# Expert layer one of a gated cross-attention and MoE block: weight block stationary, 128 moving columns, hidden rows left untransposed

## The chip, the cores and the metric

The kernel runs on one core of one Trainium2 chip. The metric is the device time of one execution in microseconds, lower is better. Three runs of the kernel before took 444.24, 444.64 and 444.83 us (median 444.64).

## What is computed

The input is 32 sequences of 128 tokens with 128 features. A cross-attention stage and a layer norm come first. What the change touches is the mixture of experts after it:

```
probs = softmax(xf @ router_w.T)
topv, topi = top_k(probs, 2); topv = topv / (topv.sum() + 1e-09)
h = gelu(einsum('td,edh->teh', xf, w1))
y = einsum('teh,ehd->ted', h, w2)
out = einsum('te,ted->td', cw, y)
x = x + tanh(g_ffn[0]) * out
```

There are 8 experts, `w1` is 128x512 and `w2` 512x128 for each, and each of the 4096 tokens goes to two of them, so there are 8192 picks. Everything is float32.

## The kernel before, in words

**Attention stage** (`each_step`, the first 55% of the time): per group of four sequences projections, scores, softmax, the product with the values, the router, and GpSimd scatters of normalised token rows into `rows`, sorted by expert. The change leaves it alone.

**Plan**: VectorE works out on the chip how many blocks of 128 rows ("slots") each expert has; `slot_row` and `slot_exp` hold the start row and the expert of each of the 71 slots (64 full ones and 7 spare). Meanwhile ScalarE rounds the first-layer weights to fp32r (`w1h`, L675) and VectorE computes the remainder `w1l = w1 - w1h` (L1013).

**Expert stage** (`each_slot`, `work` on every engine): a software pipeline over the slots. Step `8q + r` handles slot `j` in its first part and earlier slots in the others, by constants called lags. Eight steps are written out, then a rolled loop holds eight per pass, then the rest is written out. Each engine takes its work in the order of the code:

- SyncE loads 128 rows of `rows` into `xg[:, r]`, a ring of eight (L473, L479).
- TensorE, step j: transposes `xg` of slot j into `ps_x` (L1210); runs layer one of slot j-2 (L1220), three matmuls of 512 moving columns, `xh*w1h + xl*w1h + xh*w1l`, with the activations stationary and the weights moving; transposes the four 128-column blocks of `hid` of slot j-3 (L1230); runs layer two of slot j-4 (L1240), four float32 matmuls, each two weight loads and two matmul records in the profile.
- ScalarE rounds the transposed rows into `xh` (L684) and takes the gelu of `ps_score` into `hid` (L691).
- VectorE computes `xl` (L1021), copies `hidT` out of `ps_pT` (L1029, named probT in the profile since it shares that buffer), and scales the result into `yo` (L1035).
- GpSimd runs a one-element add on `pscratch` (L560) and an indirect DMA that scatters `yo` to `picked` (L569).

At `r == 0` TensorE reads the experts of the coming slots into registers (L1186), because its operands are addressed by them. `wait(pe, f_xl, j - 1)` and its like guard the buffers, of which most are double.

**Tail**: the results in `picked` are loaded back, added to `xs` by VectorE (L1043, L1045) and written out.

Of the kernel before, what the change touches and what calls it, by code (L numbers as in the profile page):

```python
# [9 lines left out]
F32R = mybir.dt.float32r  # L10
# [6 lines left out]
D = 128  # L17
# [6 lines left out]
EXPERTS = 8  # L24
HID = 512
HCH = HID // 128
# [26 lines left out]
LAG_UP = 2  # L53
LAG_HT = 3
LAG_DOWN = 4
# [74 lines left out]
def gated_cross_attention_moe(nc, x, ctxT, mask, weights, vectors, w1, w2, ident_c, tables_c,  # L130
                              integers_c, rows, picked, out):
    with ExitStack() as stack:
# [119 lines left out]

        w1h = sb("w1h", [128, EXPERTS, HID], F32R)
        w1l = sb("w1l", [128, EXPERTS, HID], F32R)
        xg = sb("xg", [128, RING, ROW])
# [26 lines left out]
        s_w1 = sem("s_w1")  # L282
        s_ffnw = sem("s_ffnw")
# [60 lines left out]
        s_w1h = sem("s_w1h")  # L344
        s_w1l = sem("s_w1l")
# [3 lines left out]
        f_xl = sem("f_xl")  # L349
        f_up = sem("f_up")  # L350
        f_gelu = sem("f_gelu")
        f_hT = sem("f_hT")
        f_hTs = sem("f_hTs")
# [31 lines left out]
        def seqs(ap):  # L385
            return ap.rearrange("p (b s) -> p b s", b=GROUP)

# [196 lines left out]
        def _(act):  # L584
# [91 lines left out]

            nc.scalar.activation(ascratch[:, :], tgates[:, :], ACT.Gelu)

            def work(q, r):
# [22 lines left out]
        def _(dve):  # L702
# [345 lines left out]
        def _(pe):  # L1048
# [130 lines left out]
            pe.wait_ge(s_w1l, EXPERTS)  # L1179
            pe.wait_ge(s_plan, PLAN)  # L1180

            def experts_of(first, count):

                at = (slot_exp[0:1, first:first + count] if isinstance(first, int)
                      else slot_exp[0:1, bass.ds(first, count)])
                _, values = nc.values_load_multi_w_load_instructions(  # L1186
                    at, engines=[mybir.EngineType.PE], min_val=0, max_val=EXPERTS - 1,
                    skip_runtime_bounds_check_because="the plan takes the minimum with the last expert")
                return [bass.ds(v, 1) for v in values]
# [3 lines left out]
            def work(q, r):  # L1193
                if r == 0:
# [5 lines left out]
                    turn["experts"] = experts_of(first, count)  # L1200
# [11 lines left out]
                if j is not None:  # L1212
# [3 lines left out]
                    e = expert(LAG_UP)  # L1216
                    pe.wait_ge(f_xl, j + 1)
                    wait(pe, f_gelu, j - 1)
                    for a, w, first in ((xh, w1h, True), (xl, w1h, False), (xh, w1l, False)):
                        last = nc.tensor.matmul(ps_score[i][:, :], a[:, (r - LAG_UP) % XRING, :],  # L1220
                                                w[:, e, :].rearrange("p o h -> p (o h)"),
                                                start=first, stop=(w is w1l))
                    last.then_inc(f_up, 1)
                j = slot_of(q, r, LAG_HT)
                if j is not None:
                    i = (r - LAG_HT) % 2
                    pe.wait_ge(f_gelu, j + 1)
                    wait(pe, f_hTs, j - 1)
                    for c in range(HCH):
# [63 lines left out]
```

## Time and profile before

| | value |
|---|---|
| runs, median (lowest to highest) | 444.64 us (444.24 to 444.83) |
| the profiled execution, first to last instruction | 452.3 us |
| PE busy | 358.2 us, 79% |
| DVE busy | 314.0 us, 69% |
| POOL busy | 244.6 us, 54% |
| ACT busy | 206.1 us, 46% |
| TensorE clock granted, mean | 0.927 |

The profile is of one execution. Its own time is known only as its span, 452.3 us, which is 7.7 us above the median of the runs without a profile; a change in time worked out in the span is carried over to the median unchanged. Busy times of different engines overlap; what bounds a stretch is read from who waits for whom in it.

### The profile page before, as it was taken

To read this page: it belongs to the slowest core of one execution; us is meant where nothing else is said; L and a number is where in the kernel's file an instruction comes from. 1 tells how busy PE (TensorE), PEld (TensorE's weight loads), DVE (VectorE), ACT (ScalarE), POOL (GpSimd) and SP (SyncE) were. 2 spreads that over 40 slices of the span, in tenths; PEclk is the share of its full clock that TensorE was granted. 3 is DMA by queue.
4 is the path that set the end of the run, shared out by engine and by line. 5 is a ranking of instruction groups with operands and counts; after the bars stand their busy time and mean duration, and the time that the engine had idled before them with its cause. 6 is when DMAs were issued, how large, how long until landed. Compare 5 with 4: busy or idle time off the path is not lost.

```text
span 452.3 us, 10441 instructions
## 1 busy us (share of the span) xinstructions
PE 358.2 (79%) x2747; PEld 287.1 (63%) x2748; DVE 314.0 (69%) x1059; ACT 206.1 (46%) x506; POOL 244.6 (54%) x302
## 2 busy tenths in 40 slices
PE   2799999989878898887553029999999999999800
PEld 2566767766565675664442018989889889898700
DVE  3778789999797997878655645655656656565545
ACT  2176667575655657556413404434333334343200
POOL 3755454528758587585467633555555555555600
PEclk9999999999999999999965559999999999999955
DMA  7224412011121011004511221212212222222079
GB/s 213 72 65 137 143 49 72 27 53 54 50 70 47 31 40 47 21 25 133 143 43 41 78 78 29 67 53 58 58 56 54 62 64 58 54 58 61 22 242 315
DMA packets 41472, 34.42 MB, mean 76 GB/s; under 512 B 5205, under 2 KB 37335, under 8 KB 41441
## 3 DMA queue, kind: packets, MB, share of 16 engines
q1 hardware_dynamic: 32898, 23.49, 18.1%
q0 software_dynamic: 4320, 8.47, 5.6%
q10 hardware_dynamic: 4224, 2.10, 1.6%
q8 instruction: 14, 0.23, 0.2%
q14 instruction: 16, 0.13, 0.1%
HBM read 22.35 MB, written 12.01 MB: 76 GB/s over the span
## 4 chain that ended last, share of the span: by engine, by line
PE 54%; DVE 16%; issue 11%; POOL 7%; DMA 6%; SPq 3%; ACT 2%; DVEq 1%; another core or an unknown queue 0%; POOLq 0%; ACTq 0%
PE ps_score L1220 9%; PE ps_score L1072 8%; PE ps_proj L1240 6%; PE ps_pT L1230 5%; PE ps_o L1240 5%; PE ps_pT L1095 4%; POOL rows L537 3%; PE ps_o L1150 3%; DMA maskbc<-picked 2%; POOL picked L569 2%; DVE rowmax L920 2%; PE ps_proj L1106 2%; PE ps_proj L1110 2%; PE ps_tail L1128 1%; DVE prob L949 1%
## 5 line engine op out<-in xcount | busy, mean ns | idle before, releaser
L523 POOL TENSOR_TENSOR kblk<-kT,tables 128x1024 f32<-128x1024 f32 x32 | 60.6, 1895 | 53.4 <-ACT kT L618 52.9
L569 POOL DMA_INDIRECT picked<-yo,xg x71 | 70.6, 994 | 11.9 <-POOL pscratch L560 11.6
L1029 DVE COPY probT<-ps_pT 128x512 f32<-128x512 f32 x71 | 49.1, 691 | 39.2 <-PE ps_pT L1230 21.9
L537 POOL DMA_INDIRECT rows<-xr,posi x64 | 64.2, 1004 | 16.1 <-issue 15.5
L1072 PE MATMUL ps_score<-kblk,qT 128*128 128x512 f32 x128 | 63.0, 605 | 9.8 <-ACT prob L634 8.4
L560 POOL TENSOR_TENSOR pscratch<-minus_half 1x1 f32<-1x1 f32 x95 | 17.6, 186 | 77.2 <-DVE yo L1035 69.5
L691 ACT ACTIVATE probT<-ps_score 128x512 f32<-128x512 f32 x71 | 42.4, 597 | 33.6 <-PE ps_score L1220 25.9
L607 ACT ACTIVATE probT<-ps_pT 128x512 f32<-128x512 f32 x64 | 35.4, 595 | 40.0 <-PE ps_pT L1095 31.3
L920 DVE TENSOR_REDUCE rowmax<-ps_score 128x4 f32<-128x512 f32 x64 | 41.8, 683 | 8.1 <-PE ps_score L1072 3.8
L1230 PE MATMUL ps_pT<-ident,probT 128*128 128x128 f32 x284 | 42.9, 274 | 0.0
L1230 PEld LDWEIGHTS ps_pT<-ident,probT 128*128 128x128 f32 x284 | 35.7, 141 | 9.8 <-issue 0.2
L1072 PEld LDWEIGHTS ps_score<-kblk,qT 128*128 128x128 f32 x128 | 22.5, 200 | 29.3 <-ACT prob L634 14.8
L638 ACT ACTIVATE prob<-prob 128x512 f32<-128x512 f32 x56 | 33.8, 630 | 9.7 <-DVE prob L949 9.4
L1240 PE MATMUL ps_proj<-w2s,probT 128*128 x288 | 38.1, 275 | 0.0
L1240 PE MATMUL ps_o<-w2s,probT 128*128 x280 | 37.0, 275 | 0.0
L949 DVE TENSOR_TENSOR prob<-ps_score,rowmax 128x512 f32<-128x512 f32 x56 | 36.1, 680 | 0.0
L1240 PEld LDWEIGHTS ps_proj<-w2s,probT 128*128 128x128 f32 x288 | 35.0, 192 | 0.1
L1220 PE MATMUL ps_score<-w1h,xh 128*128 x71 | 34.9, 491 | 0.0
L966 DVE SCALAR_TENSOR_TENSOR qT<-ps_proj,wts,maskbc 64x128 f32<-64x128 f32 x64 | 22.3, 348 | 17.7 <-ACT vals L621 11.2
L1240 PEld LDWEIGHTS ps_o<-w2s,probT 128*128 128x128 f32 x280 | 34.0, 192 | 0.0
L1095 PE MATMUL ps_pT<-ident,prob 128*128 128x128 f32 x256 | 33.2, 273 | 0.0
L684 ACT ACTIVATE xh<-ps_xT 128x128 fp32r<-128x128 f32 x36 | 10.0, 278 | 46.7 <-PE ps_xT L1210 46.7
(142 smaller groups left out, 741.5 us busy)
## 6 DMA issues: line engine op xcount, KB each, us to landing
xg<-rows SPq DMA_DIRECT2D x71, 65.0 KB, 1.8
ctxs<-ctxT SPq DMA_DIRECT2D x32, 128.0 KB, 2.1
xs<-x SPq DMA_DIRECT2D x8, 256.0 KB, 2.9
w1s<-w SPq DMA_DIRECT2D x4, 512.0 KB, 3.4
w2s<-w SPq DMA_DIRECT2D x8, 256.0 KB
w1s<-picked SPq DMA_DIRECT2D x4, 512.0 KB, 5.8
maskbc<-picked SPq DMA_DIRECT2D x4, 512.0 KB, 10.0
out<-xs ACTq DMA_DIRECT2D x8, 256.0 KB, 6.5
```

What stands on the lines that cost most here:

```text
L523: nc.gpsimd.tensor_tensor(kblk[:, r, :, :], kT[:, r, :].unsqueeze(1).broadcast_to([128, HEADS, T]), headmask.unsqueeze(2).broadcast_to([12 ...
L537: nc.gpsimd.indirect_dma_start(out=rows, out_offset=bass.IndirectOffsetOnAxis(ap=posi[:, i, pick, b:b + 1], axis=0), in_=xr[:, i, pick, b, ...
L569: nc.gpsimd.indirect_dma_start(out=picked, out_offset=bass.IndirectOffsetOnAxis(ap=xg[:, r, D + 1:D + 2].bitcast(I32), axis=0), in_=yo[:, ...
L691: nc.scalar.activation(hid[:, i, :, :], heads(ps_score[i][:, :]), ACT.Gelu).then_inc(f_gelu, 1)
L920: nc.vector.tensor_reduce(rowmax[:, r, HALF * h:HALF * (h + 1)], heads(ps_score[h][:, :]), AX.X, ALU.max).then_inc(s_max, 1)
L949: nc.vector.tensor_tensor(prob[:, r, HALF * h:HALF * (h + 1), :], heads(ps_score[h][:, :]), rowmax[:, r, HALF * h:HALF * (h + 1)].unsqueeze(2)
L1029: nc.vector.tensor_copy(hidT[:, i, :, :], heads(ps_pT[i][:, :])).then_inc(f_hTs, 1)
L1072: nc.tensor.matmul(ps_score[h][:, :], qT[:, r, h, :], flat(kblk[:, r, HALF * h:HALF * (h + 1), :]), start=True, stop=True).then_inc(s_sc, 1)
L1095: last = nc.tensor.transpose(ps_pT[h][:, j * T:(j + 1) * T], prob[:, r, HALF * h + j, :], ident[:, :])
L1220: last = nc.tensor.matmul(ps_score[i][:, :], a[:, (r - LAG_UP) % XRING, :], w[:, e, :].rearrange("p o h -> p (o h)"), start=first, stop=(w ...
L1230: last = nc.tensor.transpose(ps_pT[i][:, c * 128:(c + 1) * 128], hid[:, i, c, :], ident[:, :])
L1240: last = nc.tensor.matmul(ps_y[i][:, 0:D], hidT[:, i, c, :], w2s[:, e, c, :].rearrange("p o d -> p (o d)"), start=(c == 0), stop=(c == HCH ...
```

## The change

Layer one is turned around. A block of 128 columns of the weights is the stationary operand, and `xh` or `xl` moves with 128 columns, so that `ps_score` holds the hidden units on the partitions and the tokens along the columns. That is the layout that layer two wants as its stationary operand: the transposes of `hid`, `ps_pT` and the copy to `hidT` are gone. The three terms over four blocks are twelve matmuls. Before each, VectorE copies the expert's `w1h` and `w1l` into a small double buffer `w1c`; for that VectorE now reads `slot_exp` into its own registers at `r == 0`, and its wait for `s_w1l` stands in its own program and no longer in TensorE's. The pipeline is two steps deep and no longer four.

```diff
-LAG_UP = 2
-LAG_HT = 3
-LAG_DOWN = 4
+LAG_UP = 1
+LAG_DOWN = 2
...
+        w1c = sb("w1c", [128, 2, 2, HID], F32R)
...
         hid = probT[:, :, 0:HCH, :]
-        hidT = probT[:, :, HCH:2 * HCH, :]
...
                     act.wait_ge(f_up, j + 1)
-                    wait(act, f_hT, j - 1)
+                    wait(act, f_down, j - 1)
...
+            dve.wait_ge(s_w1l, EXPERTS)
+            turn = {}
 
             def work(q, r):
                 j = slot_of(q, r, 0)
+                if r == 0 and j is not None:
+                    first = RING * q
+                    count = min(RING, SLOTS - first) if isinstance(q, int) else RING
+                    turn["experts"] = experts_of(mybir.EngineType.DVE, first, count)
                 if j is not None:
+                    wait(dve, f_up, j - 1)
+                    for t, w in enumerate((w1h, w1l)):
+                        nc.vector.tensor_copy(
+                            w1c[:, r % 2, t, :],
+                            w[:, turn["experts"][r], :].rearrange("p o h -> p (o h)")).then_inc(f_w1, 1)
                     dve.wait_ge(f_xh, j + 1)
...
-                j = slot_of(q, r, LAG_HT)
-                if j is not None:
-                    i = (r - LAG_HT) % 2
-                    dve.wait_ge(f_hT, j + 1)
-                    wait(dve, f_down, j - 1)
-                    nc.vector.tensor_copy(hidT[:, i, :, :], heads(ps_pT[i][:, :])).then_inc(f_hTs, 1)
...
-            pe.wait_ge(s_w1l, EXPERTS)
...
                     pe.wait_ge(f_xl, j + 1)
+                    pe.wait_ge(f_w1, 2 * j + 2)
                     wait(pe, f_gelu, j - 1)
-                    for a, w, first in ((xh, w1h, True), (xl, w1h, False), (xh, w1l, False)):
-                        last = nc.tensor.matmul(ps_score[i][:, :], a[:, (r - LAG_UP) % XRING, :],
-                                                w[:, e, :].rearrange("p o h -> p (o h)"),
-                                                start=first, stop=(w is w1l))
+                    for c in range(HCH):
+                        for t, a, first in ((0, xh, True), (0, xl, False), (1, xh, False)):
+                            last = nc.tensor.matmul(
+                                ps_score[i][:, c * 128:(c + 1) * 128],
+                                w1c[:, i, t, c * 128:(c + 1) * 128],
+                                a[:, (r - LAG_UP) % XRING, :], start=first, stop=(t == 1))
                     last.then_inc(f_up, 1)
-                j = slot_of(q, r, LAG_HT)
-                if j is not None:
-                    i = (r - LAG_HT) % 2
-                    pe.wait_ge(f_gelu, j + 1)
-                    wait(pe, f_hTs, j - 1)
-                    for c in range(HCH):
-                        last = nc.tensor.transpose(ps_pT[i][:, c * 128:(c + 1) * 128], hid[:, i, c, :],
-                                                   ident[:, :])
-                    last.then_inc(f_hT, 1)
...
-                    pe.wait_ge(f_hTs, j + 1)
+                    pe.wait_ge(f_gelu, j + 1)
                     wait(pe, f_y, j - 1)
                     for c in range(HCH):
-                        last = nc.tensor.matmul(ps_y[i][:, 0:D], hidT[:, i, c, :],
+                        last = nc.tensor.matmul(ps_y[i][:, 0:D], hid[:, i, c, :],
```

How it stands in TensorE's program, one step of the rolled loop of the expert stage. Before (operands are printed as output, moving, stationary; ISA and REGISTER_ALU are register work for addresses and waits):

```order
L1210 MATMUL ps_tail<-ident,xg 128x128
L1220 ISA
L1220 MATMUL ps_score<-w1h,xh 128x512
L1220 MATMUL ps_score<-w1h,xl 128x512
L1220 REGISTER_ALU
L1220 MATMUL ps_score<-w1l,xh 128x512
L1230 MATMUL ps_pT<-ident,probT 128x128 x4
L1240 ISA
L1240 MATMUL ps_o<-w2s,probT 128x128
```

The changed program at the same place (the line numbers are those of the changed file):

```order
L1211 MATMUL ps_tail<-ident,xg 128x128
L1217 REGISTER_ALU
L1218 REGISTER_ALU
L1222 MATMUL ps_score<-xh,w1c 128x128
L1222 MATMUL ps_score<-xl,w1c 128x128
L1222 MATMUL ps_score<-xh,w1c 128x128 x2
L1222 MATMUL ps_score<-xl,w1c 128x128
L1222 MATMUL ps_score<-xh,w1c 128x128 x2
L1222 MATMUL ps_score<-xl,w1c 128x128
L1222 MATMUL ps_score<-xh,w1c 128x128 x2
L1222 MATMUL ps_score<-xl,w1c 128x128
L1222 MATMUL ps_score<-xh,w1c 128x128
```

Three matmuls of 512 columns and four transposes have become twelve matmuls of 128; the transposes that stood between layer one and layer two are gone, and layer two follows at once.

VectorE's program in the rolled loop before, two steps:

```order
L1021 TENSOR_TENSOR xl<-ps_tail,xh 128x128
L1029 COPY probT<-ps_pT 128x512
L1035 TENSOR_SCALAR yo<-ps_o,xg 128x128
L1019 REGISTER_ALU
L1021 TENSOR_TENSOR xl<-ps_xT,xh 128x128
L1029 COPY probT<-ps_pT 128x512
```

And now, at the head of the loop, with the register load of the experts and one step behind it:

```order
L390 TENSOR_LOAD slot_exp
L126 REGISTER_ALU
L1033 ISA
L1033 COPY w1c<-w1h 128x512
L1033 REGISTER_ALU
L1033 COPY w1c<-w1l 128x512
L1036 REGISTER_ALU
L126 REGISTER_ALU
L1038 TENSOR_TENSOR xl<-ps_xT,xh 128x128
L126 ISA
L1046 TENSOR_SCALAR yo<-ps_proj,xg 128x128
```

The copy out of PSUM between `xl` and `yo` is gone, and two copies from SBUF to SBUF stand ahead of `xl`, right behind `yo` of the step before.

## Rows read from the trace of the kernel before

**Rows 1.** The page: span, and the span in 40 slices for TensorE, VectorE and the clock.

```profile
span 452.3 us, 10441 instructions
...
PE   2799999989878898887553029999999999999800
...
DVE  3778789999797997878655645655656656565545
...
PEclk9999999999999999999965559999999999999955
```

**Rows 2.** Busy time by stretch: PE, PEld, DVE, ACT, POOL, then clock, DMA share, GB/s.

```profile
268.30:275.70 7.40, 7.04 (x31) 5.51 (x32) 2.74 (x7) 3.07 (x8) 0.00 (x0) 0.64 0.25 60
299.80:317.40 17.60, 17.56 (x128) 15.79 (x128) 10.52 (x24) 7.00 (x16) 9.41 (x16) 1.00 0.21 59
```

**Rows 3.** The chain of waits in one steady step of the expert stage: start us, us, what.

```profile
302.38 0.11 PE ps_tail L1210
302.49 0.70 PE ps_score L1220 x3
303.19 0.44 PE ps_pT L1230 x4
303.63 0.89 PE ps_o L1240 x8
304.52 0.11 PE ps_xT L1210
```

**Rows 4.** Timeline of weight loads around a step that began after a pause: start us, us.

```profile
282.12 0.14 PEld L1210 LDWEIGHTS ps_xT<-ident,xg 128*128 128x128 f32 x1
282.34 0.19 PEld L1220 LDWEIGHTS ps_score<-w1h,xh 128*128 128x128 f32 x1
282.45 0.19 PEld L1220 LDWEIGHTS ps_score<-w1h,xl 128*128 128x128 f32 x1
282.68 0.19 PEld L1220 LDWEIGHTS ps_score<-w1l,xh 128*128 128x128 f32 x1
```

**Rows 5.** Groups by line, 239 to 430 us: busy us, mean ns, idle before and releaser.

```profile
L1029 DVE COPY probT<-ps_pT 128x512 f32<-128x512 f32 x71 | 49.1, 691 | 39.2 <-PE ps_pT L1230 21.9 <-issue 17.2
L1240 PEld LDWEIGHTS ps_proj<-w2s,probT 128*128 128x128 f32 x288 | 35.0, 192 | 0.1
L560 POOL TENSOR_TENSOR pscratch<-minus_half 1x1 f32<-1x1 f32 x77 | 14.3, 186 | 72.2 <-DVE yo L1035 69.5 <-DVE posi L868 2.6
L1035 DVE TENSOR_SCALAR yo<-ps_proj,xg 128x128 f32<-128x128 f32 x36 | 12.6, 351 | 8.6 <-PE ps_proj L1240 8.6
L1021 DVE TENSOR_TENSOR xl<-ps_xT,xh 128x128 fp32r<-128x128 f32 x36 | 10.5, 291 | 10.2 <-ACT xh L684 8.0 <-issue 0.6
L1013 DVE TENSOR_TENSOR w1l<-w1s,w1h 128x512 fp32r<-128x512 f32 x8 | 4.9, 683 | 0.0
L569 POOL DMA_INDIRECT picked<-yo,xg x71 | 70.6, 994 | 11.9 <-POOL pscratch L560 11.6 <-issue 0.3
```

**Rows 6.** The register load of the experts on TensorE's queue: ns min/median/max.

```profile
L1186 PEldq TENSOR_LOAD <-slot_exp x10: 786/1083/1206, 264.9 to 421.8; - x10
```

**Rows 7.** VectorE groups, 0 to 240 us: SBUF to SBUF with one input.

```profile
L745 DVE TENSOR_SCALAR maskrow<-maskrow 1x4096 f32<-1x4096 f32 x1 | 2.3, 2280 | 1.4 <-DMA maskrow<-mask 1.4
L730 DVE TENSOR_SCALAR wout_g<-wts,tgates 128x256 f32<-128x256 f32 x1 | 0.4, 352 | 2.5 <-ACT tgates L586 2.5
```

**Rows 8.** Timeline, before and in the fill of the expert stage: start us, us.

```profile
259.86 4.90 DVE L1013 TENSOR_TENSOR w1l<-w1s,w1h 128x512 fp32r<-128x512 f32 x8
...
268.36 0.48 PE L1210 MATMUL ps_xT<-ident,xg 128*128 128x128 f32 x1 [15.01 <-DMA xg<-rows]
...
269.18 0.29 DVE L1021 TENSOR_TENSOR xl<-ps_xT,xh 128x128 fp32r<-128x128 f32 x1 [4.42 <-ACT xh L684]
...
271.19 0.41 PE L1210 MATMUL ps_tail<-ident,xg 128*128 128x128 f32 x1
...
272.68 1.03 PE L1230 MATMUL ps_pT<-ident,probT 128*128 128x128 f32 x4
273.53 0.29 PE L1210 MATMUL ps_xT<-ident,xg 128*128 128x128 f32 x1
```

**Rows 9.** Timeline, last input transpose and last layer-two group.

```profile
419.11 0.27 PE L1210 MATMUL ps_xT<-ident,xg 128*128 128x128 f32 x1
...
426.78 1.13 PE L1240 MATMUL ps_proj<-w2s,probT 128*128 x8
```

**Rows 10.** Timeline: VectorE SBUF ops beside a GpSimd multiply, then beside its indirect DMA.

```profile
87.71 1.90 POOL L523 TENSOR_TENSOR kblk<-kT,tables 128x1024 f32<-128x1024 f32 x1 [0.97 <-ACT kT L618]
87.80 1.83 DVE L946 TENSOR_SCALAR nmax<-rowmax 128x4 f32<-128x4 f32 x1
...
209.31 1.15 DVE L984 TENSOR_SCALAR x2n<-xs,nm,rs 128x128 f32<-128x128 f32 x4
...
209.70 1.01 POOL L537 DMA_INDIRECT rows<-xr,posi  x1 [0.16 <-issue]
```

More of the change, by code:

```diff
@@ L251, in gated_cross_attention_moe @@
         pad_row = sb("pad_row", [128, EXPERTS], I32)
+        xg = sb("xg", [128, RING, ROW])
         w1h = sb("w1h", [128, EXPERTS, HID], F32R)
         w1l = sb("w1l", [128, EXPERTS, HID], F32R)
-        xg = sb("xg", [128, RING, ROW])
         xh = sb("xh", [128, XRING, 128], F32R)
         xl = sb("xl", [128, XRING, 128], F32R)
+        w1c = sb("w1c", [128, 2, 2, HID], F32R)
         yo = sb("yo", [128, RING, D])
         hid = probT[:, :, 0:HCH, :]
-        hidT = probT[:, :, HCH:2 * HCH, :]
         yb = [half.rearrange("p (g b k d) -> p g b k d", b=GROUP, k=2, d=D)[:, g]
@@ L282, in gated_cross_attention_moe @@
         s_w1 = sem("s_w1")
+        s_w1h = sem("s_w1h")
+        s_w1l = sem("s_w1l")
         s_ffnw = sem("s_ffnw")
@@ L343, in gated_cross_attention_moe @@
         s_plan = sem("s_plan")
-        s_w1h = sem("s_w1h")
-        s_w1l = sem("s_w1l")
         f_load = [sem(f"f_load{i}") for i in range(RING)]
@@ L349, in gated_cross_attention_moe @@
         f_xl = sem("f_xl")
+        f_w1 = sem("f_w1")
         f_up = sem("f_up")
         f_gelu = sem("f_gelu")
-        f_hT = sem("f_hT")
-        f_hTs = sem("f_hTs")
         f_down = sem("f_down")
@@ L386, in seqs, with experts_of @@
             return ap.rearrange("p (b s) -> p b s", b=GROUP)
+        def experts_of(engine, first, count):
+            at = (slot_exp[0:1, first:first + count] if isinstance(first, int)
+                  else slot_exp[0:1, bass.ds(first, count)])
+            _, values = nc.values_load_multi_w_load_instructions(
+                at, engines=[engine], min_val=0, max_val=EXPERTS - 1,
+                skip_runtime_bounds_check_because="the plan takes the minimum with the last expert")
+            return [bass.ds(v, 1) for v in values]
         block = stack.enter_context(nc.Block())
@@ L1178, in _ @@
             pe.wait_ge(s_ffnw, 16 * EXPERTS)
-            pe.wait_ge(s_w1l, EXPERTS)
             pe.wait_ge(s_plan, PLAN)
[L1182 to L1189, printed above, removed]
             turn = {}
@@ L1199, in work @@
                         count = min(RING * q + RING - LAG_UP, SLOTS) - first
-                    turn["experts"] = experts_of(first, count)
+                    turn["experts"] = experts_of(mybir.EngineType.PE, first, count)
                     turn["first"] = 0 if isinstance(q, int) and q == 0 else -LAG_DOWN
@@ L1215, in work @@
                     i = (r - LAG_UP) % 2
-                    e = expert(LAG_UP)
                     pe.wait_ge(f_xl, j + 1)
+                    pe.wait_ge(f_w1, 2 * j + 2)
                     wait(pe, f_gelu, j - 1)
-                    for a, w, first in ((xh, w1h, True), (xl, w1h, False), (xh, w1l, False)):
-                        last = nc.tensor.matmul(ps_score[i][:, :], a[:, (r - LAG_UP) % XRING, :],
-                                                w[:, e, :].rearrange("p o h -> p (o h)"),
-                                                start=first, stop=(w is w1l))
-                    last.then_inc(f_up, 1)
-                j = slot_of(q, r, LAG_HT)
-                if j is not None:
-                    i = (r - LAG_HT) % 2
-                    pe.wait_ge(f_gelu, j + 1)
-                    wait(pe, f_hTs, j - 1)
-                    for c in range(HCH):
-                        last = nc.tensor.transpose(ps_pT[i][:, c * 128:(c + 1) * 128], hid[:, i, c, :],
-                                                   ident[:, :])
-                    last.then_inc(f_hT, 1)
+                    for c in range(HCH):
[4 more added lines that the diff above has]
+                                a[:, (r - LAG_UP) % XRING, :], start=first, stop=(t == 1))
+                    last.then_inc(f_up, 1)
                 j = slot_of(q, r, LAG_DOWN)
```

## The prediction

> **What bounds the kernel now.** I read the page first: span and slices. TensorE is above 90% busy in every slice of the expert stage, VectorE at five to six tenths, and the clock is full there except in the first steps [rows 1]. Then busy time by stretch: in 17.6 us, eight steps, TensorE is busy for 17.56 us, VectorE for 10.52, GpSimd for 9.41, ScalarE for 7.00 [rows 2]. Then the chain of waits: a steady step is a closed run of TensorE work, 0.11 for the input transpose, 0.70 for layer one, 0.44 for the four transposes of `hid`, 0.89 for layer two, 2.14 us in all [rows 3]. So TensorE's own work bounds the stage, and what counts is what a step costs there; the others have about 0.8 us to spare in each. The attention stage and the tail are untouched.
>
> What bounds TensorE inside a step differs by matmul. Three matmuls of 512 columns in 0.70 us are 0.233 each, 0.020 over 512 columns at 2.4 GHz (0.213): their moving side bounds. The records of 128 columns in layer two come every 0.112 (0.89 / 8) [rows 3]. The decisive row is a weight load with nothing before it to hide it. In a step that began after a pause, the load for `xl*w1h` starts 0.11 us behind the load for `xh*w1h`, and the third only 0.23 later, when the second matmul starts [rows 4]. So a load of 128 fp32r columns takes about 0.11 us at full clock, twice what 128 moving columns need (0.053). The loads of layer two look the same (192 ns against 0.19) and their records come at the same pace [rows 4, 5]. With 512 columns the load is hidden; with 128 it is the longer half.
>
> **The change, term by term.**
>
> TensorE, a steady step. Gone: 3 x 0.233 = 0.70 and four transposes, 0.44; together 1.14. Added: twelve pairs of load and matmul. Their spacing is not in the trace. From below it is bounded by the moving side, 0.233 - 384 / 2400 MHz = 0.073; from above by the float32 price of the same shape, two records, 0.223. I take 0.112, the pace of layer two, because its weight loads have the same form and length and are as long as its moving side: 12 x 0.112 = 1.34. The step becomes 0.11 + 1.34 + 0.89 = 2.34, **0.20 more than now**. The moving columns are as many as before in layer one, 3 x 512; it is the twelve exposed loads that cost more than the transposes saved.
>
> The number of steps. Between the fourth and the last input transpose (slots 3 and 70) lie 67 full steps: 67 x 0.20 = **+13.4 us**. The register load at the head of each pass (about 1.08 us [rows 6], of which 17.6 - 8 x 2.14 = 0.5 shows) stays as it is.
>
> Filling. The first transpose starts at 268.36, when its DMA lands, and the first `xl` is done at 269.5. Layer one of slot 0 can then start. The clock is at 1.2 GHz until about 273.5, where four transposes take 0.85 instead of 0.44 [rows 8]; so twelve pairs take 2.6, to 272.1; transpose 2 takes 0.2; half of layer one of slot 1 takes 1.3 at the low clock and half 0.7 at the full one, to 274.3; layer two of slot 0 ends at 275.1. There transpose 3 starts, which now starts at 271.19: **+3.9**. This is because two lags instead of four put the first layer two ahead of it.
>
> Draining. From the last input transpose to the end of layer two now 419.11 to 427.9, 8.8 us [rows 9]. Then: a step of 2.34, layer one of slot 70 and two layers two, 1.34 + 2 x 0.89, a register load that shows 0.5, and 0.2 for the last matmul to leave: 6.2. **-2.6**.
>
> VectorE. Gone is a copy from PSUM (0.69 [rows 5]). Added are two copies SBUF to SBUF, 128x512. One-input operations there take 352 ns for 256 columns and 2280 for 4096, 0.50 ns a column: 128x512 would be about 0.48 [rows 7]; the upper bound is `w1l`'s 0.68, which come 0.61 apart [rows 5, 8]. A step has 2 x 0.48 + 0.29 + 0.35 = 1.6, at most 2.0, under 2.34: hidden. Behind the copies on its queue stand `xl` and then `yo`; for `xl` of slot j TensorE waits a step later. VectorE's new register load, if like TensorE's 1.08, comes once in eight steps: from the end of a step 0.55 to the end of `yo`, 1.1, two copies 1.0 to 1.2 and `xl` 0.3 are 3.0 to 3.2, against 2.34 + 0.5 + 0.11 = 2.95 at which layer one needs it. Part of the load runs while `yo` does, so I count nothing, and at most 0.3 x 8 = 2 us for the range. If that cover fails, `xl` is late and layer one waits.
>
> GpSimd has 0.18 + 0.16 + 0.99 = 1.33 of 2.34 [rows 5]. ScalarE is unchanged; the gelu of slot j-1 follows layer one and is needed a step later. On SyncE's queue the loads wait for the scatter of eight slots before, which now comes two steps after its transpose and not four: more slack. TensorE no longer waits for `w1l`, which was done at 264.8, long before 268.36: nothing [rows 8].
>
> Sum: +13.4 + 3.9 - 2.6 = **+14.7 us**. Against the profiled execution 452.3 + 14.7 = 467.0; that execution is 7.7 above the median, and the difference carries over: 444.64 + 14.7 = **459.3 us**.
>
> Bounds of the likeliest case: with the loads at 0.108 instead of 0.112 and the register loads all hidden (8 x 0.5), 453. With the 0.020 that a 512-column fp32r matmul takes over its columns added to each pair, 0.132 x 12 = 1.58, a step of 2.58: +29.5 + 1.8, 476.
>
> **The rivals.**
>
> *Loads overlap after all (faster).* The place is the same twelve pairs. If the next load ran while the one before was still waiting for its matmul, the moving side would bound at 0.073: 0.88 for layer one, a step of 1.88, 67 x -0.26 = -17.4, filling +3.0, draining -3.6: 427. It decides from a pair spacing under about 0.095 (1.14 / 12). For it speaks that VectorE could follow at 1.6. Against it speak the two loads 0.11 apart after a pause, and that no loads in the steady expert stage come closer [rows 4]. The Trainium skill, TensorE: Matmul & The Clock Gate, section Back-to-back issue gap, gives about 81 ns for a sustained stream of load and matmul at 128 columns; by that figure layer one would be 0.97, and the kernel, as an estimate, near 434. The same page's formula for a weight load, columns over 1.2, gives 107 ns for 128, and with that the trace agrees (0.11).
>
> *A locked port.* VectorE's SBUF copies and GpSimd could exclude each other. A one-input VectorE operation of 4 columns beside a GpSimd multiply took 1.83 us, until that ended [rows 10]; so there is such a lock. If the indirect DMA's instruction held it too, VectorE's chain would be yo 0.35, copy 0.48, GpSimd 1.33, copy 0.48, xl 0.29 = 2.93: a step 0.79 longer than now, 67 x 0.79 + 1.2 = +54, 499. Against it: four such VectorE operations took 1.15 us beside an indirect DMA, 0.26 apart with the DMA begun in their middle [rows 10]. The Trainium skill, SBUF — State Buffer, section Who interferes with whom, says that a one-input copy in its two-port mode and GpSimd lock each other out, descriptor writing included; the trace agrees for GpSimd's arithmetic and shows nothing of it for the indirect DMA.
>
> *The float32 price.* If the chip ran fp32r with few moving columns as float32, a pair would be 0.223: 2.68, a step of 3.68, 67 x 1.54 = 103 plus some 5 for filling and draining: 553. No row shows fp32r under 512 columns. The built program holds one load and one matmul for each term, where a float32 matmul has two.
>
> *The clock falls.* Layer one would keep the array's moving side busy for half its time. At 1.2 GHz throughout, as in the filling [rows 2, 8], a step would be 4.7 and the kernel about 625. But the attention stage has slices of 70 to 80% at full clock [rows 1].
>
> **How the numbers follow.** Likeliest case 0.81, overlap 0.08, lock 0.05, float32 price 0.04, clock 0.02. The range 453 to 476 is the likeliest case with its bounds, 0.81; adding a further case would stretch it by 20 us or more for a few hundredths. About 0.2% is what a measurement of this kernel can tell from no change. Only the overlap case is faster, with an edge of it near zero: faster 0.07, same 0.01, slower 0.92.
>
> **What would show it.** Twelve weight loads of layer one about 0.11 apart and their matmuls too, layer one 1.34 in the chain; steps of 2.34; TensorE still above 90% busy at full clock; the two copies under 0.5 each and VectorE idle before `yo`, waiting for layer two; transpose 3 near 275. Wrong would be: TensorE idle before layer one with VectorE's `w1c` or `xl` named, copies of 1 us or more beside the indirect DMA, or a spacing far from 0.11.

## The result, and the profile after

The changed kernel takes 465.3 us (median of four runs, 465.02 to 467.63); the kernel before, on the same chip, 444.44. The ratio is 1.0496, 95% interval 1.0447 to 1.0545: **slower by 20.9 us**, where 14.7 were forecast. The time lies in the range of 453 to 476.

The page of the changed kernel, span and slices, against [rows 1]:

```profile
span 463.2 us, 11185 instructions
...
PE   2799999989989898976430699999999999999900
...
DVE  3668789999899999898558254554545545455435
...
PEclk9999999999999999999555599999999999999955
```

TensorE is as full as before and VectorE a little emptier. The two spans, 463.2 and 452.3, differ by 10.9 us only, because the attention stage was 10.0 us longer in the profiled execution of before: the first transpose of the expert stage starts at 268.36 there [rows 8] and at 258.32 here. So I compare the expert stage alone, from that transpose to the end of the last layer two: 159.6 us before, 181.0 after, **+21.4**, which is what the runs show. This is the chain of waits in it, against [rows 3]:

```profile
316.56 0.11 PE ps_tail L1211
316.67 1.29 PE ps_score L1222 x12
317.96 0.94 PE ps_o L1234 x8
318.90 0.83 issue
319.73 0.32 PE ps_xT L1211
320.06 1.43 PE ps_score L1222 x12
321.49 0.94 PE ps_proj L1234 x8
```

A steady step is 0.11 + 1.29 + 0.94 = 2.34, the forecast to the hundredth: twelve pairs of layer one and eight records of layer two share 2.23. What was not forecast is the piece "issue" of 0.83 at the head of the pass. The same place in the kernel before:

```profile
316.48 0.89 PE ps_o L1240 x8
317.37 0.08 issue
317.46 0.32 PE ps_xT L1210
317.78 0.85 PE ps_score L1220 x3
```

There it is 0.08. The slow restart behind it (0.32 for the transpose, layer one 0.14 longer) is in both. The register loads of `slot_exp`, against [rows 6]:

```profile
L390 PEldq TENSOR_LOAD <-slot_exp x10: 310/2238/2312, 248.9 to 436.3; - x10
L390 DVEq TENSOR_LOAD <-slot_exp x9: 594/600/1073, 253.8 to 419.0; - x9
```

TensorE's takes 2.2 us for nine registers, where it took 1.1 for ten. In the pass above it ran from 317.29 to 319.49: its queue was 1.6 us ahead of the array's work (which ended at 318.90), the rest of the load shows, and work resumes 0.24 later.

The groups by line, against [rows 5]:

```profile
L1222 PEld LDWEIGHTS ps_score<-xh,w1c 128*128 128x128 f32 x568 | 94.3, 197 | 1.1 <-DVE xl L1038 0.6
L576 POOL DMA_INDIRECT picked<-yo,xg x71 | 70.9, 999 | 11.8 <-POOL pscratch L567 11.5
L567 POOL TENSOR_TENSOR pscratch<-minus_half 1x1 f32<-1x1 f32 x95 | 23.8, 251 | 90.7 <-DVE yo L1046 84.9
L1046 DVE TENSOR_SCALAR yo<-ps_proj,xg 128x128 f32<-128x128 f32 x36 | 12.6, 351 | 42.7 <-PE ps_proj L1234 42.7
L1033 DVE CAST w1c<-w1h 128x512 fp32r x71 | 31.5, 444 | 10.8 <-issue 8.6
```

The weight loads have the form and length of those in layer two; the copies take 0.42 in a steady step (0.44 is the mean); VectorE waits for TensorE ahead of every `yo`, and TensorE for VectorE hardly at all; the indirect DMA takes 999 ns beside the copies, 994 before [rows 5].

Busy time by stretch, columns as in [rows 2]: the filling, what follows it, and eight steady steps.

```profile
258.30:267.90 9.60, 9.30 (x42) 8.78 (x43) 3.19 (x11) 2.19 (x6) 0.45 (x2) 0.50 0.18 42
267.90:275.00 7.10, 7.10 (x66) 7.10 (x65) 3.14 (x11) 2.62 (x6) 3.52 (x6) 1.00 0.17 49
299.80:318.60 18.80, 18.79 (x167) 18.73 (x168) 9.71 (x31) 6.99 (x16) 9.88 (x15) 1.00 0.18 49
```

TensorE runs at 1.2 GHz for 9.6 us from its first transpose; before it was 5.2, from 268.3 to 273.5.

The +21.4 by part. Steps are counted from one input transpose to the next; "heads" is what the two steps at the eight pass heads take over a steady one.

| part of the expert stage | before | after | measured | forecast |
|---|---|---|---|---|
| 67 steady steps | 2.143 each | 2.343 each | +13.4 | +13.4 |
| eight pass heads | 3.3 | 9.4 | **+6.1** | 0 |
| filling, transpose 0 to 3 | 2.83 | 8.29 | +5.5 | +3.9 |
| draining, transpose 70 to the end | 8.80 | 5.73 | -3.1 | -2.6 |
| rest (by difference) | | | -0.5 | |

### The profile page after: what moved, and what is told of

It reads as the page before. It is cut to its first block, busy times and chain, and to the rows that moved or that the text cites. A ratio compares the mean times of both kernels' runs of the same rounds, so it can differ in the third digit from the quotient of the medians.

```text
span 463.2 us, 11185 instructions
## 1 busy us (share of the span) xinstructions
PE 374.7 (81%) x3102; PEld 317.4 (69%) x3103; DVE 308.6 (67%) x1131; ACT 205.9 (44%) x506; POOL 250.9 (54%) x302
## 4 chain that ended last, share of the span: by engine, by line
PE 55%; DVE 20%; issue 11%; DMA 5%; ACT 3%; POOL 2%; SPq 2%; DVEq 1%; POOLq 0%; ACTq 0%
PE ps_score L1222 21%; PE ps_proj L1234 7%; PE ps_o L1234 7%; PE ps_score L1083 5%; DVE rowmax L926 3%; PE ps_pT L1106 3%; DMA maskbc<-picked 2%; DVE prob L955 2%; POOL rows L544 2%; DVE qT L972 2%; PE ps_proj L1117 2%; PE ps_proj L1121 2%; PE ps_xT L1211 1%; PE ps_o L1161 1%; DMA vecs<-vectors 1%
## 5 line engine op out<-in xcount | busy, mean ns | idle before, releaser
L1222 PE MATMUL ps_score<-xh,w1c 128*128 128x128 f32 x568 | 111.8, 284 | 0.3 <-DVE xl L1038 0.3
L1222 PEld LDWEIGHTS ps_score<-xh,w1c 128*128 128x128 f32 x568 | 94.3, 197 | 1.1 <-DVE xl L1038 0.6
L1222 PE MATMUL ps_score<-xl,w1c 128*128 128x128 f32 x284 | 79.5, 280 | 0.0
L567 POOL TENSOR_TENSOR pscratch<-minus_half 1x1 f32<-1x1 f32 x95 | 23.8, 251 | 90.7 <-DVE yo L1046 84.9
L544 POOL DMA_INDIRECT rows<-xr,posi x64 | 64.2, 1003 | 16.1 <-issue 14.7
L1222 PEld LDWEIGHTS ps_score<-xl,w1c 128*128 128x128 f32 x284 | 55.9, 197 | 0.0
L1046 DVE TENSOR_SCALAR yo<-ps_proj,xg 128x128 f32<-128x128 f32 x36 | 12.6, 351 | 42.7 <-PE ps_proj L1234 42.7
L1234 PE MATMUL ps_proj<-w2s,probT 128*128 x288 | 40.8, 286 | 0.0
L1033 DVE CAST w1c<-w1h 128x512 fp32r x71 | 31.5, 444 | 10.8 <-issue 8.6
L1234 PE MATMUL ps_o<-w2s,probT 128*128 x280 | 38.7, 281 | 0.0
L645 ACT ACTIVATE prob<-prob 128x512 f32<-128x512 f32 x56 | 33.9, 630 | 10.5 <-DVE prob L955 9.8
L1046 DVE TENSOR_SCALAR yo<-ps_o,xg 128x128 f32<-128x128 f32 x35 | 12.3, 351 | 39.3 <-PE ps_o L1234 39.3
```

What stands on the lines that cost most here:

```text
L544: nc.gpsimd.indirect_dma_start(out=rows, out_offset=bass.IndirectOffsetOnAxis(ap=posi[:, i, pick, b:b + 1], axis=0), in_=xr[:, i, pick, b, ...
L645: last = nc.scalar.activation(flat(p), flat(p), ACT.Exp, scale=SCALE)
L1033: nc.vector.tensor_copy(w1c[:, r % 2, t, :], w[:, turn["experts"][r], :].rearrange("p o h -> p (o h)")).then_inc(f_w1, 1)
L1222: last = nc.tensor.matmul(ps_score[i][:, c * 128:(c + 1) * 128], w1c[:, i, t, c * 128:(c + 1) * 128], a[:, (r - LAG_UP) % XRING, :], start ...
L1234: last = nc.tensor.matmul(ps_y[i][:, 0:D], hid[:, i, c, :], w2s[:, e, c, :].rearrange("p o d -> p (o d)"), start=(c == 0), stop=(c == HCH ...
```

## The experiments

Three questions: whether the pace of the pairs is that of the weight load, what makes the pass heads dear, and whether VectorE's new work costs anything. Every time stands beside runs of the kernel before on the same chip. Two chips gave it 442.7 and 443.1 us, a third 455.5; across chips only ratios compare. Spans and steps are from the trace.

### What a pair waits for

**256 moving columns.** The same twelve weight loads, each followed by twice the moving columns, taken from `w1c` itself, so layer one computes something else.

```diff
-                                ps_score[i][:, c * 128:(c + 1) * 128],
+                                ps_score[i][:, c % 2 * 256:c % 2 * 256 + 256],
...
-                                a[:, (r - LAG_UP) % XRING, :], start=first, stop=(t == 1))
+                                w1c[:, i, t, 0:256], start=first, stop=(t == 1))
```

> Each of the twelve matmuls of layer one moves 256 columns of w1c instead of 128 columns of xh or xl, so layer one's result is another; weight loads, copies and waits stay. Theory L (the pair is bound by its weight load of 0.112 us): 256 columns take 0.107, the pair 0.112 to 0.13, a step 2.34 to 2.55, 465 to 480 us. Rival M (the pair is bound by its moving side plus some 0.06 us for each matmul): 0.112 + 0.053 = 0.165 a pair, a step of 2.98, about 509 us.

467.2 us, ratio 1.055 (1.0473 to 1.0627). The chain of waits:

```profile
301.78 0.11 PE ps_xT L1211
301.89 1.43 PE ps_score L1222 x12
303.32 0.89 PE ps_proj L1234 x8
```

A step is 2.43. Twice the moving columns cost 0.09 of a step, 0.007 a pair (1.43 / 12 = 0.119 where the chain and the step gave 0.112). Were a pair bounded by the time its moving columns take, twice the columns would have doubled it. It is bounded by something that doesn't grow with them. One rival fits this run as well: that fewer than 256 fp32r columns move at half pace. The weight loads shown with the next run bear on it.

**bfloat16 operands in layer one.** `w1h`, `w1l`, `xh`, `xl` and `w1c` in bfloat16, three terms as before; all else as in the change. The terms carry fewer bits than fp32r's.

```diff
-        w1h = sb("w1h", [128, EXPERTS, HID], F32R)
-        w1l = sb("w1l", [128, EXPERTS, HID], F32R)
+        w1h = sb("w1h", [128, EXPERTS, HID], BF16)
+        w1l = sb("w1l", [128, EXPERTS, HID], BF16)
...
-        w1c = sb("w1c", [128, 2, 2, HID], F32R)
+        w1c = sb("w1c", [128, 2, 2, HID], BF16)
```

> The change with both operands of layer one in bfloat16 (high and low half, three terms as before): w1h, w1l, w1c, xh and xl are bfloat16, the same twelve pairs of 128 columns. Theory L (the load of a 4-byte weight block bounds the pair at 0.112): with 2-byte weights the load is half as long, the pair 0.055 to 0.08, layer one 0.7 to 0.96, a step 1.7 to 1.96, 420 to 438 us. Rival F (a fixed cost of each pair, for decoding or for the change of weights): the pair stays at 0.11 and the time within 3 us of 465.

424.7 us, ratio **0.9579** (0.9538 to 0.962). The chain of waits, up to the head of a pass:

```profile
286.87 0.11 PE ps_tail L1211
286.98 0.67 PE ps_score L1222 x12
287.65 0.95 PE ps_o L1234 x8
288.60 1.57 issue
290.17 0.33 PE ps_xT L1211
```

Its weight loads, and those of layer two in the same stretch (busy us, mean ns):

```profile
L1222 PEld LDWEIGHTS ps_score<-xh,w1c 128*128 128x128 bf16 x487 | 39.9, 98 | 0.5
L1234 PEld LDWEIGHTS ps_o<-w2s,probT 128*128 128x128 f32 x248 | 30.2, 192 | 0.0
```

The same twelve pairs take 0.67, 0.056 each, half of fp32r's, and the load's record is 98 ns long instead of 197. That is the pace of the moving side (0.053), so the load is hidden. Both operands changed type here. What tells the weight load from the moving side is the start of layer one after a pause, when no queued work holds the loads. First the change, then bfloat16:

```profile
319.93 0.19 PEld L1222 LDWEIGHTS ps_score<-xh,w1c 128*128 128x128 f32 x1
320.04 0.19 PEld L1222 LDWEIGHTS ps_score<-xl,w1c 128*128 128x128 f32 x1
...
306.04 0.10 PEld L1222 LDWEIGHTS ps_score<-xh,w1c 128*128 128x128 bf16 x1
306.07 0.10 PEld L1222 LDWEIGHTS ps_score<-xl,w1c 128*128 128x128 bf16 x1
```

The second load starts 0.11 behind the first in fp32r, and it does so whether 128, 256 or 512 columns move (the change, the run before this one, [rows 4]); in bfloat16 it starts 0.03 behind. So those 0.11 us are the load's, and no slow moving side is needed for a pair of 0.112. **In fp32r the pair is bounded by its weight load; in bfloat16, where a load holds up the next for 0.03, by its moving side.** The Trainium skill, TensorE: Matmul & The Clock Gate, section Weight-path perf modes, says that a fast weight load is on when 128 weights are loaded and the type is not FP32; the two rows agree if fp32r counts as FP32. The 81 ns of its section Back-to-back issue gap is seen for neither type: 112 and 56.

**The kernel before without the transposes.** To see what the change bought, I left the transposes of `hid` and VectorE's copy out of the kernel before, so layer two works on untransposed data.

```diff
-                    for c in range(HCH):
-                        last = nc.tensor.transpose(ps_pT[i][:, c * 128:(c + 1) * 128], hid[:, i, c, :],
-                                                   ident[:, :])
-                    last.then_inc(f_hT, 1)
...
-                    nc.vector.tensor_copy(hidT[:, i, :, :], heads(ps_pT[i][:, :])).then_inc(f_hTs, 1)
...
-                        last = nc.tensor.matmul(ps_y[i][:, 0:D], hidT[:, i, c, :],
+                        last = nc.tensor.matmul(ps_y[i][:, 0:D], hid[:, i, c, :],
```

> The kernel before with the four transposes of hid and the copy to hidT taken out; layer two reads hid as it is, so its result is that of a wrong matrix. Layer one keeps 512 moving columns, the lags 2 and 4 stay. Theory L: a step is 0.11 + 0.70 + 0.89 = 1.70, 0.44 less, 31 us less than the kernel before, about 412; this is the whole that the transposes can be worth, and twelve pairs cost 0.64 a step against it. Rival (VectorE or GpSimd bounds below 2.1): a step above 1.8 and TensorE idle ahead of layer two.

422.9 us, ratio 0.954 (0.948 to 0.96): 20 us gained, 11 less than expected. Most steps without a pause are 1.70 to 1.8 long, near what was expected. The others are longer: between the fourth and the last input transpose TensorE pauses 17 times, 8.1 us in all (7 times and 0.8 us in the kernel before), and starts again slowly each time. This is who waits for whom from 280 to 390 us:

```profile
PE ps_xT L1203 <- issue: 2.5, 4, 0.7
PE ps_xT L1203 <- DMA xg<-rows: 2.1, 6, 0.7
PE ps_tail L1203 <- DMA xg<-rows: 1.2, 2, 1.0
POOL pscratch L559 <- DVE yo L1028: 32.7, 55, 1.6
```

Over the stage 5.6 of the 8.1 us are waits for the rows of `xg`. In this kernel, with its lag of four, a buffer of `xg` is loaded again only after the scatter of eight slots before. GpSimd waits for `yo` in every step, so its own work of 1.33 us is not shown to be a bound. Neither limit is seen in the bfloat16 kernel with its lag of two: no wait for rows in its steady steps of 1.73.

### What a pass head costs

At `r == 0` the kernel before loads ten registers from `slot_exp[8q - 4]`, the changed one nine from `slot_exp[8q - 2]`. Two theories of the load's length: it goes with the number of registers, or (A) with where the first stands, since 8q - 4 is a multiple of four and 8q - 2 is not. The expectations call the two together C. Against them stand Q (the load ends a fixed time behind the work queued ahead of it) and S (something in the changed step holds it). The alternative for the whole head is (D): VectorE's new register load makes `xl` late.

**Eight registers instead of nine**, from the same start.

```diff
-                    count = RING - LAG_UP + LAG_DOWN
+                    count = RING
```

> TensorE's register load at the head of each pass reads 8 experts (from slot 8q-2) instead of 9, of which the ninth is never used. In the changed kernel the load takes 2.2 us in the rolled passes, in the kernel before 1.08 us for 10, and TensorE's array is empty for about 1.0 us there. Theory C (the count or the alignment of what is read sets the load's length): the load falls to 1.1 us or less, and 6 us come back over eight passes: about 459. Rival Q (the load ends a fixed time behind the work queued ahead of it): unchanged, within 1 us of 465. Rival D (VectorE's own load holds it): unchanged too.

463.6 us, ratio 1.0499 (1.0425 to 1.0574). The load takes 1.99 us, 0.25 less for one register less, and the pause at the head shrinks from 0.83 to 0.65. The number counts, at 0.25 a register, but ten of them took 1.08 before: number alone does not explain it, and the load of 1.1 that was expected did not come. The heads take 2.1 us less than in the change, which the time does not show beyond its interval.

**The load placed behind layer one** of the same step, unchanged itself.

```diff
             def work(q, r):
-                if r == 0:
-                    first = RING * q - LAG_DOWN if not isinstance(q, int) or q > 0 else 0
...
                     last.then_inc(f_up, 1)
+                if r == 0:
+                    first = RING * q - LAG_DOWN if not isinstance(q, int) or q > 0 else 0
...
                 j = slot_of(q, r, LAG_DOWN)
```

> TensorE's register load stands behind layer one of the step instead of ahead of its input transpose; only layer two needs the registers. Theory Q (the load waits for queued array work and then takes some 0.6 us in which the array is empty): the gap only moves behind layer one, 465 within 2 us. Theory C or any in which the load runs beside queued work: layer one's 1.34 us lie over it, the heads of the passes cost 0 to 0.5 us in place of 1.2, 457 to 460.

461.4 us, ratio 1.0418 (1.036 to 1.0477). The load still takes 2.2 us, and TensorE now pauses ahead of layer two:

```profile
321.04 1.15 PE L1235 MATMUL ps_proj<-w2s,probT 128*128 x8 [0.45 <-issue]
```

A pass costs 0.67 over steady steps instead of 1.25: half of it is the place. Theory Q, by which it would have stayed, falls.

**VectorE without its register load**; the copies stay, at a fixed expert for each slot of the ring, so layer one takes other weights than it should.

```diff
-                    turn["experts"] = experts_of(mybir.EngineType.DVE, first, count)
...
-                            w[:, turn["experts"][r], :].rearrange("p o h -> p (o h)")).then_inc(f_w1, 1)
+                            w[:, r, :]).then_inc(f_w1, 1)
```

> VectorE copies the block of expert r, fixed, so it loads no registers; the copies and everything else stay. The result is that of wrong experts in layer one. Theory D (VectorE's register load makes xl and w1c late at the head of a pass, or holds TensorE's load): the heads of the passes fall from 1.2 to 0.5 us over eight steps' worth, about 459. Theories C and Q: TensorE's load stays at 2.2 us and the time within 1.5 us of 465.

466.9 us, ratio 1.0533 (1.0466 to 1.06). No gain, and the heads are the same to 0.02. Theory D falls for the changed kernel as it stands.

**An aligned start**: ten registers from 8q - 4, as in the kernel before; else only the offset by which the registers are counted follows.

```diff
-                    first = RING * q - LAG_DOWN if not isinstance(q, int) or q > 0 else 0
-                    count = RING - LAG_UP + LAG_DOWN
+                    first = RING * q - 4 if not isinstance(q, int) or q > 0 else 0
+                    count = 10
```

> The change with TensorE's register load as the kernel before has it: ten experts from slot 8q-4, 16-byte aligned, in place of nine from slot 8q-2. Durations so far: ten from 8q-4 1.08 us; nine from 8q-2 2.2; eight from 8q-2 2.0; on VectorE eight from 8q 0.60 and seven from 64 1.07; three 0.79, one 0.31. Theory A (from a 16-byte aligned start four are read at a time in about 0.3, others singly in 0.24): the load is 1.08, the heads of the passes cost 0.4 to 0.6 in place of 1.2, 5 to 6 us come back: about 460. Theory S (something in the changed step's work holds the load, whatever it reads): 2.2 us and 465.

461.95 us, ratio 1.0407 (1.034 to 1.0474). One register more, and the load takes half the time:

```profile
L390 PEldq TENSOR_LOAD <-slot_exp x10: 786/1084/1434, 247.9 to 432.4; - x10
```

Theory A holds, and S falls, since the changed step is the same. But a pass still costs 0.64 over steady steps, and not at the same place: the pause ahead of the transpose is down to 0.1, and layer one of the step after waits. The chain of waits there runs over VectorE:

```profile
318.52 0.05 DVE yo L1046
...
318.67 0.24 issue
...
319.02 0.60 DVEq L390
...
320.10 0.37 issue
320.47 0.41 DVE w1c L1033
320.88 0.21 DVE xl L1038
321.09 0.23 issue
321.31 0.30 PE ps_score L1222
```

This is the lateness that theory D named. Behind TensorE's longer pause it was hidden; with that gone, the chain names it as the next bound, 0.6 a pass with the slow restart. I did not run a kernel with both loads gone, so its price is read from the chain and not shown by a run.

The load is not all of that lateness. At a pass head the first copy starts beside GpSimd's indirect DMA; in the change:

```profile
319.72 0.99 POOL L576 DMA_INDIRECT picked<-yo,xg  x1 [0.16 <-POOL pscratch L567]
...
320.26 0.70 DVE L1033 CAST w1c<-w1h 128x512 fp32r x1 [0.97 <-issue]
```

It takes 0.70 where a steady step's takes 0.42, and ends 0.25 after the DMA. All eight copies of the change that started 0.38 to 0.46 before the end of such a DMA ended 0.25 behind it; in the bfloat16 run with the aligned load it is 0.12. In a steady step both copies start before the DMA, and keep their 0.42. So 0.28 of the lateness comes with where the load pushes the copy to.

**Both edits**, aligned and behind layer one:

```diff
                     last.then_inc(f_up, 1)
+                if r == 0:
+                    first = RING * q - 4 if not isinstance(q, int) or q > 0 else 0
+                    count = 10
...
                 j = slot_of(q, r, LAG_DOWN)
```

> As align10, and the load stands behind layer one of the step. With the load at 2.2 us and that place the heads cost 0.66. Theory A: 1.08 us fit under layer one's 1.34, the heads cost 0 to 0.1, about 9 us less than the change: 455 to 457. Theory S: as pe_load_late, 461.

459.2 us, ratio 1.0366 (1.0328 to 1.0405): the best fp32r form, and the only one whose interval lies clear of the change's (1.0447 to 1.0545); for the others the gain is read from the trace. It is some 3 us above the 455 to 457 expected, since the heads did not go to 0.1. A pass costs 0.64 here too, and the wait named at each is that for `xl`. So of the change's 20.9 us it has some 5 back; 16 stay, 13.4 of them the pairs.

| kernel | TensorE's load, us | a pass over eight steady steps, us | 1.2 GHz after the first transpose, us |
|---|---|---|---|
| before | 1.08 | 0.44 | 5.2 |
| the change | 2.24 | 1.25 | 9.6 |
| eight registers | 1.99 | 1.02 | 10.4 |
| load behind layer one | 2.18 | 0.67 | 14.8 |
| VectorE's load gone | 2.2 | 1.26 | 14.4 |
| aligned | 1.08 | 0.64 | 14.4 |
| aligned, behind | 1.08 | 0.64 | 10.5 |

The last column is one reason why the runs gain less or more than the heads say: it differs from run to run by up to 5 us of low clock, about 2.5 us of time. What sets it is not shown.

### The copies, and two ways with bfloat16

These ran on the chip where the kernel before takes 455.5 us.

**No copies.** `w1c` is filled once ahead of the loop; VectorE has neither copies nor a register load, and every slot uses the same experts' weights.

```diff
-                    for t, w in enumerate((w1h, w1l)):
-                        nc.vector.tensor_copy(
-                            w1c[:, r % 2, t, :],
...
-                    pe.wait_ge(f_w1, 2 * j + 2)
+                    pe.wait_ge(f_w1, 4)
```

> VectorE fills both halves of w1c once, from experts 0 and 1, ahead of the loop; the two copies a step and VectorE's register load are gone, so layer one uses wrong experts for most slots. If the copies are hidden, as VectorE's 1.4 us of 2.34 in a step says: steps of 2.34 still, 463 to 466. Rival (the copies or their wait delay xl or the matmuls): steps under 2.3, below 460.

477.2 us, ratio 1.0483 (1.0403 to 1.0563), against 1.0496 with the copies. Steps of 2.34, as expected, and passes 1.12 over steady. The copies and VectorE's register load together cost 0.13 us a pass in the change.

**bfloat16 with the aligned load behind layer one**, the edits of the two runs above put together:

```diff
-        w1c = sb("w1c", [128, 2, 2, HID], F32R)
+        w1c = sb("w1c", [128, 2, 2, HID], BF16)
...
                     last.then_inc(f_up, 1)
+                if r == 0:
+                    first = RING * q - 4 if not isinstance(q, int) or q > 0 else 0
+                    count = 10
```

> bf16_copy with TensorE's register load of ten from slot 8q-4 and behind layer one. In bf16_copy the step is 1.73 and the heads of the passes cost 1.83 each. Theory A: the load is 1.1 us, 0.67 of it under layer one, the heads cost 0 to 0.8: 7 to 14 us less than 424.7, so 411 to 418. If GpSimd's chain of add and indirect DMA (1.33 us and 0.3 of issue) bounds at 1.7 instead, no less than 411.

430.25 us, ratio **0.9469** (0.9385 to 0.9552): faster than both kernels, with 1.73 a step and 0.86 a pass where bfloat16 alone had 1.82. The intervals of the two bfloat16 runs (0.9469 here, 0.9579 there, on different chips) just overlap; the expert stage in the trace is 134.6 us against 140.4. On the chip of bfloat16 alone the ratio would give 419.5 us, a little above the 411 to 418 expected: at the heads TensorE still pauses 0.2 ahead of layer two and 0.3 for `xl`, and two passes took 0.7 and 1.1 more, with waits of 0.5 and 0.9 for ScalarE's gelu. It is the version I would hand on, if three bfloat16 terms are precise enough for the layer.

**bfloat16 without `w1c`:** the stationary side is addressed in `w1h` and `w1l` by TensorE's registers; no copies, twelve registers loaded from an aligned start.

```diff
-                                w1c[:, i, t, c * 128:(c + 1) * 128],
+                                (w1h, w1l)[t][:, e, c * 128:(c + 1) * 128].rearrange("p o h -> p (o h)"),
```

> Layer one in bfloat16 with the stationary block addressed by register in w1h and w1l: no w1c, no copies, no register load on VectorE; TensorE loads twelve experts from slot 8q-4, three aligned groups of four, at the head of the pass and ahead of the input transpose. Theory A: that load is about 0.9 to 1.0 us and the heads cost 0.3 to 0.8: 412 to 418. Rival (a register-held stationary address costs sequencer time on each pair, some 0.12 us for each of eight blocks): layer one 1.0 to 1.5 us in place of 0.67, steps of 2.0 to 2.5, 440 to 475.

443.5 us, ratio 0.975 (0.9691 to 0.981), 13 us slower than with the copies. Layer one is 0.67 as there, but the step is 1.90, and 67 x 0.17 is 11. The timeline of weight loads shows where it goes; here, between layer one and layer two:

```profile
303.57 0.10 PEld L1213 LDWEIGHTS ps_score<-xh,w1l 128*128 x1
303.79 0.97 PEld L1225 LDWEIGHTS ps_o<-w2s,probT 128*128 128x128 f32 x8
```

and with the copies:

```profile
304.05 0.10 PEld L1214 LDWEIGHTS ps_score<-xh,w1c 128*128 128x128 bf16 x1
304.11 0.97 PEld L1235 LDWEIGHTS ps_proj<-w2s,probT 128*128 128x128 f32 x8
```

0.16 us more in every step. A pass of eight steps holds 109 instructions of register and address work on TensorE instead of 53; its queue no longer keeps ahead. The heads fit that: they cost 1.4 a pass, though the load takes 0.85 and VectorE has none. That reading is argued from the count and the gaps, not tested by itself. Neither expectation came: on that chip the ratio gives 432 us, between the 418 of one and the 440 of the other. VectorE's copies were the cheap way.

**The kernel before once more**, with a profile.

> The kernel before once more with a profile, to see how much of the distance between the first profile of it (span 452.3) and its runs (444) lies in the attention stage. Expert stage 159 to 160 us as in the first profile, from the first input transpose to the end of layer two; the attention stage shorter by up to 10 us, as in all profiles of the other kernels, where the first transpose starts at 256 to 259 instead of 268.4.

454.2 us, span 452.4, first transpose at 267.7, expert stage 160.0 us. The attention stage was not shorter, against the expectation; this chip is the one where the kernel takes 455.5. The first profile (span 452.3, 268.36, 159.6) is like this one. In all nine profiles of the other kernels on the faster chips the first transpose starts at 256.6 to 258.6. So its excess of 7.7 us over the median very likely lay ahead of the expert stage; no profile of the kernel before at 444 us shows it.

## Why the prediction was right, and where not

**What bounds:** right. TensorE's own work bounds every step before and after; the chain names nothing else between pass heads.

**The steady step, +0.20:** right to the hundredth, 67 x 0.20 = 13.4, and for the reason given: the two weight loads 0.11 apart after a pause [rows 4]. The runs with 256 moving columns and with bfloat16 showed it from both sides, and the first loads after a pause separate it from a slow moving side.

**"The register load at the head of each pass ... stays as it is":** this is the term that failed. It was priced at a change of nothing and measured **+6.1 us**, nearly all of what was missing (20.9 - 14.7 = 6.2). I looked at the load's duration [rows 6] and not at its operands: the shorter pipeline moved its first register from slot 8q - 4 to 8q - 2, and the load doubled, from 1.08 to 2.24, though it reads one register less. The mechanism of the term (a load that shows as far as the queue's lead doesn't cover it) was right; what it had to hide had changed. The aligned run puts 0.6 of the 0.8 us that a pass costs more down to the start of the load, about 4.9 of the 6.1 us; the rest stays with it, by the chain on VectorE's side.

**Filling, +3.9:** direction right, +5.5 measured. The sum let the clock rise 5.2 us after the first transpose, as it had before; it rose after 9.6, so that the whole filling ran at 1.2 GHz. In the changed kernel and its six fp32r variants on chips of the same speed, that time ran from 3.6 to 14.8 us, so it was no quantity to take from one trace to a tenth; it belonged in the range. Why it differs stays open.

**Draining, -2.6:** right, -3.1.

**VectorE:** the copies at 0.48 took 0.42, 0.70 beside the end of an indirect DMA, and are hidden in steady steps. For the register load I counted nothing, and at most 0.3 x 8 for the range: right for the change, but only since TensorE's own pause covered it. Once that went, VectorE's chain cost 0.6 a pass, about twice my bound. Its load takes 0.60 and not TensorE's 1.08.

**The range:** that 465.3 fell inside it is in part luck. Its upper end, 476, was opened for a longer spacing of the pairs (0.132), which did not come; the pass heads and the filling, 7.7 us over their terms, used that room, less 1.0 for draining and the rest. The lower end by its own terms (0.048 x 67 = 3.2 and 8 x 0.5 = 4) is 452, not 453.

**Rivals:** overlapping loads are out, with 0.112 measured for a pair and a 256-column pair at 0.119. The locked port is out as it was priced: steps are 2.34 and the indirect DMA takes 999 ns with two copies in every step. But something of it exists: a copy started some 0.4 us before the end of an indirect DMA ended 0.25 us after it, and took 0.70 for 0.42. The order of the steady step keeps the copies clear of that stretch; at the pass heads it costs 0.28. The float32 price and the falling clock are out, with the same 0.112 and full clock in the steady steps. The carry-over from the profiled execution to the median held, as far as its excess lay ahead of the stage concerned.

## What to carry to other kernels

With 128 moving columns each 4-byte stationary block costs its load, 0.112 us, so turning a matmul round to save transposes pays only if the loads added (twelve here, for 1.14 us of work removed) cost less than what goes. With 2-byte operands the whole was 5% faster than the fp32r kernel before; the kernel before in bfloat16, the fair match, was not run. When a pipeline's depth changes, look at everything indexed by it: a load of nine registers from a start that is no multiple of four took twice as long as one of ten from a multiple of four. And a term "hidden behind" something that you mean to shorten has to be priced again for after that.

## What the runs showed that I had not expected

- **Register loads.** Of consecutive 4-byte integers: eight from a multiple of four take 0.60 us, ten 1.08, twelve 0.85; eight from two beyond it 1.99, nine 2.24. All fit, within 0.05, 0.30 for each group of four and 0.24 for each one left over, and 0.25 for every one where the start is not aligned. One alone takes 0.31, three from slot 68 take 0.79 (0.72 by the fit), and an engine's first load took up to 0.5 more than the fit.
- **The clock at the start of the stage** rose 3.6 us after the first transpose with 256 moving columns, 5.2 in the kernel before, and 9.3 to 14.8 in the fp32r forms with 128, though TensorE was busy for 9.30 of 9.60 us there.
- **TensorE's register-held stationary addresses** in every pair: the bfloat16 kernel with them took 13 us more than the one that copies 2 x 512 columns per slot on VectorE.
- **A copy beside an indirect DMA.** VectorE's copy is not held up where the DMA starts during it (0.42), but one that started some 0.4 us before the DMA's end ended 0.25 us after the DMA, in all eight cases.
